# Gates carried with the sorted rows, and expert products added into the residual rows by the gather's own transfer

## The reference

```
xn     = layernorm(x) * gamma + beta
probs  = softmax(xn @ router_w.T / 1.5)          # 8 experts
w, idx = top_k(probs, 2)                         # the two gates of a token
y[e]   = silu(xn @ W1[e]) @ W2[e]                # 128 -> 512 -> 128
out    = w[0] * y[idx[0]] + w[1] * y[idx[1]] + x
```

## Time and profile before

| | us |
|---|---|
| median of 3 runs | 1152.73 |
| lowest and highest run | 1149.02, 1153.8 |
| the profiled execution's own time | 1139.17 |
| its span, first to last instruction | 1137.3 |
| DVE busy in the span | 935.6 (82%) |
| PE busy | 908.5 (80%) |
| POOL busy | 846.0 (74%) |
| ACT busy | 841.1 (74%) |
| mean granted TensorE clock | 0.877 of full speed |

### The profile page before, as it was taken

The page is one execution under the profiler, slowest core; times in us unless marked ns, Lnnn a source line. Parts: engine busy times, 40 slices in busy tenths (PEclk is TensorE's granted clock), DMA queues, the critical chain, the costliest instruction groups (busy, mean ns, idle before and its releaser), DMA issues. The chain is left out here.

```text
span 1137.3 us, 27887 instructions
## 1 busy us (share of the span) xinstructions
PE 908.5 (80%) x8522; PEld 726.7 (64%) x8522; DVE 935.6 (82%) x2425; ACT 841.1 (74%) x2706; POOL 846.0 (74%) x1144
## 2 busy tenths in 40 slices
PE   2487877879889788978889778978889888978681
PEld 1255555657678576766677566767677676768571
DVE  0499998889998899899999899889999899955132
ACT  1499988688887788788888788787888778853130
POOL 3389978788778888698778988798878986781503
PEclk9579788778998899889999899889999799988696
DMA  3703400533246623482237523582237523246562
GB/s 100 177 10 98 108 1 16 140 100 117 84 122 176 182 76 108 132 246 88 75 122 186 174 74 108 156 238 71 77 120 198 154 73 113 87 147 198 172 215 61
DMA packets 117045, 139.38 MB, mean 123 GB/s; under 512 B 11042, under 2 KB 99490, under 8 KB 116898
## 3 DMA queue, kind: packets, MB, share of 16 engines
q1 hardware_dynamic: 112802, 129.21, 38.3%
q0 software_dynamic: 4096, 8.40, 2.6%
HBM read 107.81 MB, written 29.75 MB: 121 GB/s over the span
## 5 line engine op out<-in xcount | busy, mean ns | idle before, releaser
L700 ACT ACTIVATE exps<-scores,neg_max 128x512 f32<-128x512 f32 (+3 forms) x1024 | 542.9, 551 | 102.1 <-DVE neg_max L989 101.1
L989 DVE TENSOR_REDUCE neg_max<-scores 128x1 f32<-128x512 f32 (+3 forms) x896 | 423.4, 524 | 51.3 <-PE scores L1119 49.1
L627 POOL TENSOR_TENSOR exps<-exps 128x512 f32<-128x512 f32 x256 | 326.7, 1276 | 21.4
L623 POOL TENSOR_SCALAR exps<-exps,inv_l,lam_l 128x384 f32<-128x384 f32 (+3 forms) x448 | 272.7, 615 | 87.2 <-DVE inv_l L964 75.6
L1151 PE MATMUL trans<-ident,exps 128*128 128x128 f32 x1280 | 234.6, 313 | 91.3 <-ACT diffT L707 69.3
L1117 PE MATMUL scores<-stack 72*128 72x512 bf16 (+3 forms) x1024 | 272.6, 335 | 16.6 <-DMA stack<-parts_dram 15.6
L1151 PEld LDWEIGHTS trans<-ident,exps 128*128 128x128 f32 x1280 | 158.4, 158 | 155.3 <-issue 95.3
L700 ACT ACTIVATION_READ_ACCUMULATOR exps<-scores,neg_max 128x1 f32 x1024 | 235.8, 230 | 0.0
L999 DVE TENSOR_REDUCE abs_sum<-exps 128x1 f32<-128x512 f32 (+3 forms) x448 | 222.8, 520 | 8.8 <-POOL exps L627 8.8
L707 ACT ACTIVATE diffT<-trans 128x512 f32<-128x512 f32 x320 | 196.4, 614 | 35.1 <-PE trans L1151 34.3
L1119 PE MATMUL scores<-causal_bf,ident_bf 128*128 128x128 bf16 x1024 | 209.0, 237 | 0.0
(11 more groups left out here) (138 smaller groups left out, 921.6 us busy)
## 6 DMA issues: line engine op xcount, KB each, us to landing
w_sb<-w_dram SPq DMA_DIRECT2D x120, 512.0 KB, 3.8
stack<-parts_dram SPq DMA_DIRECT2D x288, 96.0 KB
parts_dram<-parts SPq DMA_DIRECT2D x104, 128.0 KB
xg<-x_sorted_dram SPq DMA_DIRECT2D x24, 256.0 KB, 4.2
y_sorted_dram<-y_sorted SPq DMA_DIRECT2D x24, 256.0 KB, 4.5
x_in<-x_dram SPq DMA_DIRECT2D x8, 256.0 KB, 4.7
x_res<-x_dram SPq DMA_DIRECT2D x8, 256.0 KB, 4.8
o_dram<-y_out SPq DMA_DIRECT2D x8, 256.0 KB, 2.3
```

Source lines behind the costliest of these rows:

```text
L623: nc.gpsimd.tensor_scalar(diff[:, ring, col:col + w], exps[:, ring, 1, col:col + w], inv_l2[:, i:i + 1], lam_l1[:, i:i + 1], ALU.mult, ALU ...
L627: nc.gpsimd.tensor_tensor(diff[:, ring, :], diff[:, ring, :], exps[:, ring, 0, :], ALU.subtract)\
L700: nc.scalar.activation(exps[:, ring, k, col:col + w], scores[:, c % 2, k, col:col + w], ACT.Exp, bias=neg_max[:, c % 2, k, i:i + 1], accum ...
L989: nc.vector.tensor_reduce(neg_max[:, c % 2, k, i:i + many], scores[:, c % 2, k, col:col + many * w].rearrange("p (i w) -> p i w", w=w), AX ...
```

## The change

Five things are changed, and all slots of the tasks that remain stay where they were.

- `xh` holds each row twice, 129 numbers wide: one copy for each of the two choices, the last number being that choice's gate. DVE writes the first copy (L889), ACT makes the second (new instruction behind `xnT`), and routing step 15 writes the gates into column 128 of both.
- Rows of `x_sorted` and `xg` are 129 numbers (516 bytes) instead of 128 (512 bytes). The scatter waits for ACT's copy and for routing step 15. SP's load of `xg` waits until all 15 products of the batch before are copied, since the gates in `xg` are read by those copies.
- ACT's copy of the product to `y_sorted` takes its scale from `xg[:, j, 128]`, one number per partition, where it had none.
- The gather adds into `x1_twice` (`compute_op=ALU.add`), which has three buffers in place of two. Gathers 4 to 7 wait for gathers 0 to 3, which add into the same rows.
- The 64 combines, `y_back`, `acc` and `gates` are gone. "norm3" waits for gathers 4 to 7.

```diff
-        xh = sb("xh", [P, NT, D])
+        xh = sb("xh", [P, TOP, NT, D + 1])
-        xg = sb("xg", [P, TILES, D])
+        xg = sb("xg", [P, TILES, D + 1])
-        x1_twice = sb("x1_twice", [P, 2, NT, D])
-        acc = sb("acc", [P, NT, D])
+        x1_twice = sb("x1_twice", [P, 3, NT, D])
...
                     sp.wait_ge(scattered.sem, scattered.after(n, TOP * NT))
-                    sp.wait_ge(turned.sem, turned.after(n - 1, len(CHUNKS)))
+                    sp.wait_ge(y_copied.sem, y_copied.after(n - 1, TILES))
...
-                                pool.wait_ge(xh_done.sem, xh_done.after(n, 1))
+                                pool.wait_ge(xh_copied.sem, xh_copied.after(n, 1))
+                                pool.wait_ge(route_step.sem, route_step.after(n, ROUTE_STEPS))
                             nc.gpsimd.indirect_dma_start(
                                 x_sorted[n % 2][:, :], bass.IndirectOffsetOnAxis(ap=place_int[:, n % 2, i:i + 1], axis=0),
-                                xh[:, i % NT, :], None).then_inc(scattered.sem, 16)
+                                xh[:, i // NT, i % NT, :], None).then_inc(scattered.sem, 16)
...
-                                pool.wait_ge(combined.sem, combined.after(n - 1, TOP * NT))
+                                pool.wait_ge(acc_set.sem, acc_set.after(n, 1))
+                            if i >= NT:
+                                pool.wait_ge(gathered[i - NT].sem, gathered[i - NT].after(n, 1))
                             nc.gpsimd.indirect_dma_start(
-                                y_back[:, i, :], None, y_dram[n % 2][:, :],
-                                bass.IndirectOffsetOnAxis(ap=place_int[:, n % 2, i:i + 1], axis=0)).then_inc(gathered[i].sem, 16)
+                                x1_twice[:, n % 3, i % NT, :], None, y_dram[n % 2][:, :],
+                                bass.IndirectOffsetOnAxis(ap=place_int[:, n % 2, i:i + 1], axis=0),
+                                compute_op=ALU.add).then_inc(gathered[i].sem, 16)
...
+                            act.wait_ge(xh_done.sem, xh_done.after(n, 1))
+                            nc.scalar.activation(xh[:, 1, :, 0:D], xh[:, 0, :, 0:D], ACT.Copy).then_inc(xh_copied.sem, 1)
...
-                            nc.scalar.activation(y_sorted[:, c % 2, j % NT, :], bank[:, 0:D], ACT.Copy)\
+                            nc.scalar.activation(y_sorted[:, c % 2, j % NT, :], bank[:, 0:D], ACT.Copy, scale=xg[:, j, D:D + 1])\
...
-                    dve.wait_ge(combined.sem, combined.after(n - 2, TOP * NT))
-                    i = nc.vector.tensor_scalar(gates[:, n % 2, :, :], top[:, :, :], 0.5, None, ALU.mult)
+                    i = nc.vector.tensor_scalar(xh[:, :, :, D], top[:, :, :], 0.5, None, ALU.mult)
...
-                        if name == "combine":
-                            i = task[2]
-                            t = i % NT
-                            dve.wait_ge(gathered[i].sem, gathered[i].after(n, 1))
...
                         if name == "norm3":
-                            dve.wait_ge(combined.sem, combined.after(n, TOP * NT))
-                            moments(1, acc).then_inc(last_moments.sem, 1)
+                            for i in range(NT, TOP * NT):
+                                dve.wait_ge(gathered[i].sem, gathered[i].after(n, 1))
+                            moments(1, x1_twice[:, n % 3, :, :]).then_inc(last_moments.sem, 1)
```

More of the change, by code:

```diff
@@ L92 @@
 GATHER_SLOTS = (82, 83, 85, 85, 87, 88, 88, 90)
-COMBINE_SLOTS = (86, 86, 88, 90, 91, 91, 91, 93)
 STACK_SLOT = 33
@@ L156, in _place @@
                         ("expert", EXPERT_SLOTS), ("y_out", Y_OUT_SLOTS), ("scatter", SCATTER_SLOTS),
-                        ("gather", GATHER_SLOTS), ("combine", COMBINE_SLOTS)):
+                        ("gather", GATHER_SLOTS)):
         for i, slot in enumerate(slots):
@@ L240, in build @@
         scratch = nc.dram_tensor("parts_dram", [3, NH, len(STORED), HD, T], BF16).ap()
-        x_sorted = [nc.dram_tensor(f"x_sorted{i}_dram", [TILES * P, D], FP32).ap() for i in range(2)]
+        x_sorted = [nc.dram_tensor(f"x_sorted{i}_dram", [TILES * P, D + 1], FP32).ap() for i in range(2)]
         y_dram = [nc.dram_tensor(f"y_sorted{i}_dram", [TILES * P, D], FP32).ap() for i in range(2)]
@@ L350, in build @@
         gathered = [pool_dma(f"gathered{i}", 1) for i in range(TOP * NT)]
-        combined = signal("combined", TOP * NT)
+        xh_copied = signal("xh_copied", 1)
         inv_spread = signal("inv_spread", 1)
@@ L936, in body @@
                                                            op0=ALU.add, op1=ALU.mult).then_inc(hidden_done.sem, 1)
-                        if name == "combine":
-                            i = task[2]
-                            t = i % NT
-                            dve.wait_ge(gathered[i].sem, gathered[i].after(n, 1))
-                            dve.wait_ge(route_step.sem, route_step.after(n, ROUTE_STEPS))
-                            dve.wait_ge(acc_set.sem, acc_set.after(n, 1))
-                            dve.wait_ge(y_done.sem, y_done.after(n - 1, 1))
-                            if i >= NT:
-                                dve.wait_ge(combined.sem, combined.after(n, t + 1))
-                            nc.vector.scalar_tensor_tensor(
-                                out=acc[:, t, :], in0=y_back[:, i, :], scalar=gates[:, n % 2, i // NT, t:t + 1],
-                                in1=acc[:, t, :] if i >= NT else x1_twice[:, n % 2, t, :],
-                                op0=ALU.mult, op1=ALU.add).then_inc(combined.sem, 1)
                         if name == "norm3":
-                            dve.wait_ge(combined.sem, combined.after(n, TOP * NT))
-                            moments(1, acc).then_inc(last_moments.sem, 1)
+                            for i in range(NT, TOP * NT):
+                                dve.wait_ge(gathered[i].sem, gathered[i].after(n, 1))
+                            moments(1, x1_twice[:, n % 3, :, :]).then_inc(last_moments.sem, 1)
                         if name == "finish":
@@ L955, in body @@
                             dve.wait_ge(last_rstd.sem, last_rstd.after(n, 1))
-                            normalise(y_out, acc, 1, 2).then_inc(y_done.sem, 1)
+                            normalise(y_out, x1_twice[:, n % 3, :, :], 1, 2).then_inc(y_done.sem, 1)
                     for n, c in chunks(b, stages, slot, LAG_EXP + 1):
@@ L1059, in side_task @@
                     for t in range(NT):
-                        last = nc.tensor.transpose(bank[:, t * P:(t + 1) * P], xh[:, t, :], ident[:, :])
+                        last = nc.tensor.transpose(bank[:, t * P:(t + 1) * P], xh[:, 0, t, 0:D], ident[:, :])
                 if name == "logits":
@@ L1085, in side_task @@
                     for i, j in enumerate(c):
-                        last = nc.tensor.transpose(bank[:, i * P:(i + 1) * P], xg[:, j, :], ident[:, :])
+                        last = nc.tensor.transpose(bank[:, i * P:(i + 1) * P], xg[:, j, 0:D], ident[:, :])
                 if name == "hidden":
```

6 lines of the change are left out of this document (2 added, 4 removed).

## The result

| | before | after |
|---|---|---|
| median of nine runs, us | 1152.73 | 1159.52 |
| ratio, 95% interval | | 1.008 [1.0055, 1.0105] |
| the profiled execution's own time, us | 1139.17 | 1156.72 |
| its span, us | 1137.3 | 1154.8 |
| mean granted clock | 0.877 | 0.869 |

By the ratio the change made the kernel 0.8% slower, some 9 us; the two medians lie 6.8 us apart. In two later sets of runs the same kernel gave 1.0043 [1.0016, 1.0071] and 1.0071 [1.0047, 1.0095]. I had forecast 0.6% faster, so the prediction was wrong in its sign.

The account below looks back on a forecast made before the run. A body was taken as DVE's work plus one PE stall for `xg`, the end as a latency chain. -16.0 + 3 + 3 + 1 + 1.6 + 0.3 = -7.1 us gave 1145.5 us on the median (-0.62%), range 1133 to 1170.

Parts of the forecast that it names:

- The combines, -16.0: In the five bodies with attention, DVE without its combines saves 3.2 of 3.8 us a body: -16.0 us.
- The gather that adds, +1 in the bodies and +1.6 at the end: POOL takes 1.2 us per gather instead of 1.00: +1 us over five bodies, +1.6 for the last eight.
- mostly POOL's to absorb: In the gather window of a body, 6 x 0.2 us extra would mostly vanish in POOL: +1 for five.
- the adding gather makes POOL the bound: Rival: at 2.04 us a gather, POOL needs 39.7 us in a 37 us stretch; +20.6, 1173.6 us; chance 0.16.
- its switching point of 1.5: Gather time on POOL from which that rival's sum is slower than before: extra price x = 0.5 us.
- its formula: That rival's sum over five bodies and the end, x the extra gather price: 5 (6x - 5.1) + 8x + 6.3.
- DVE's busy time falls by about 29 us: Sign that the forecast is right: DVE, whole kernel, loses about 29 us of busy time.
- The end, +1.6 and +0.3: Final chain: eight dearer gathers +1.6; landing +0.6, last combine gone -0.35, product copy 0.09 later, together +0.3.
- Rows of 516 bytes, +3: Load of `xg`, which PE awaits, takes 0.5 us longer in five bodies and the drain: +3 us.
- ACT, +3: ACT's scaled product copy and second `xh` copy, mostly covered by its waits for DVE: 0.4 us a body, +3.
- New waits, 0: Added waits of SP's load, the scatter, gathers 4 to 7 and norm3 were to cost nothing.

## Why the prediction was wrong

- **The combines, -16.0.** Too large by a third: -11.0 for their removal alone. What holds the rest is not shown. PE's transposes wait for POOL already in the kernel before (58.4 and 21.1 us, rows that I left out), but with the combines gone these waits did not rise (58.8 and 19.1); DVE's wait for scores did, from 49.1 to 53.9 us.
- **The gather that adds, +1 in the bodies and +1.6 at the end.** This step failed, and it turned the sign. I took 1.2 us between bounds of 1.00 and 2.04; it was 1.585. And I had called the extra time "mostly POOL's to absorb", +1 us for five bodies. POOL did not absorb it: the extra 0.59 us stand eight times in a body, PE's transposes wait for POOL, and the five bodies took 618 to 622 us where they took 606 and 607 with plain gathers. By the ratios it is some 10 us for the 64, and POOL kept busy for as long costs the same. The rival "the adding gather makes POOL the bound" was the right one, and the 1.585 us lie beyond its switching point of 1.5. But its formula gives only 5 (6 x 0.59 - 5.1) + 8 x 0.59 + 6.3 = +3.2 us, since it still let each body win 1.6 us, by half a slot that POOL would absorb, and the five together won nothing. "DVE's busy time falls by about 29 us" was wrong: it fell by 16, and by 21 and 20 with plain gathers.
- **The end, +1.6 and +0.3.** The mechanism held: 8 times the extra price, 4.7 us, and a landing 0.7 us longer (3.30 against 2.57).
- **Rows of 516 bytes, +3.** The size was near (+5.5 [1.8, 9.2]), by luck, as the place was wrong. The load of `xg`, on which I had put it, did not change. I had overlooked the two clearing stores at the start, which carry rows of `xg` too. By the rule of the Trainium skill ("DMA: Bandwidth & Descriptors", section "How a descriptor splits into AXI transactions") I had worked out 1.28 times (642 / 32 = 20 beats against 16 are 1.25; with the last beat of each row counted in full it is 20.5, and 1.28). The stores took 10.3 / 6.6 = 1.56 times and the load no more than before, so neither fits the estimate. Nor do rows of 576 bytes: by the same rule they start off a 256-byte boundary three times in four and take 21 beats on average, an estimate of 1.31 times, and the stores took 7.1 / 6.6 = 1.08 times. Why a pitch of 516 bytes is slow to store is open.
- **ACT, +3.** The durations were near (406 ns for 406, 654 for 614), and no price shows. I take it as covered by ACT's waits for DVE.
- **New waits, 0.** Right. Gathers 4 to 7 did not wait at the end, and neither scatter nor load came later by the rows. (The slots of the third pair, 85 and 88, are three apart and not five; a landing of 3.4 us still fits.)

## What to carry to other kernels

Taking work from the busiest engine by giving it to a transfer is only free if the engine that issues the transfer has room: price the issue instruction first, and look at who already waits for that engine. An engine that falls behind by a slot also changes which instructions run side by side, and two that get in each other's way can then give back busy time that was saved. And when rows change their length, follow every transfer that carries them, the one at the very start too.

## What the hardware showed that I had not expected

- An indirect gather of 128 rows of 512 bytes that adds holds POOL 1585 ns, a plain one 995; it makes 11264 packets in the software queue for 64 gathers and 64 scatters in place of 4096, while the median landing is 3.4 us in place of 3.3.
- Stores to HBM of 967.5 KB with a row pitch of 516 bytes landed after 10.1 to 10.7 us (10.6 to 11.3 behind the first load of `x`); 960 KB at 512 took 6.6 to 6.7, and 1080 KB at 576 took 7.1. Loads of four tiles at the pitch of 516 landed after 4.1 to 4.8 us where the profiles give it, 4.2 at 512.
- One DVE `TENSOR_SCALAR` of 128x128 took 1286 ns in place of 343 while POOL's 128x512 `TENSOR_TENSOR` ran for 1.40 us. How much of such busy time becomes time of the kernel, no run here could tell.
